# Layer 3 cross attention: TensorE's step loop written out, key parts held twice, weighted sums in one piece

## The reference

```python
q = (q_input @ W_Q + b_Q).reshape(B, LQ, 16, 8).transpose(0, 2, 1, 3)
k = (kv_input @ W_K + b_K).reshape(B, LK, 16, 8).transpose(0, 2, 1, 3)
v = (kv_input @ W_V + b_V).reshape(B, LK, 16, 8).transpose(0, 2, 1, 3)
sim = einsum('bhqd,bhkd->bhqk', q, k) / sqrt(8)
sim = where(key_padding_mask, neg_inf, sim)
out = einsum('bhqk,bhkd->bhqd', softmax(sim, axis=-1), v)
return out.reshape(B, LQ, 128) @ W_O + b_O
```

## Time and profile before

| what | us |
|---|---|
| median of 3 runs | 1829.14 |
| lowest and highest run | 1823.56, 1829.15 |
| the profiled execution, its own time | 1828.54 |
| its span in the trace | 1826.8 |
| busy in it: TensorE matmul | 1546.7 (85%) |
| busy: VectorE, ScalarE, GpSimd | 1257.7 (69%), 834.4 (46%), 321.7 (18%) |
| layer 3's steps, first row product to last weighted sum | from 1200.7 to 1673 |

### The profile page before, as it was taken

How to read it: one execution, slowest core, us unless ns; L and a number is a source line. 1 busy time by engine, 2 the same in 40 slices (tenths; PEclk the granted TensorE clock), 3 DMA queues, 4 the chain that set the end, 5 groups by cost and what they waited for, 6 DMA issues and landing times. The chain is left out here.

```text
span 1826.8 us, 40229 instructions
## 1 busy us (share of the span) xinstructions
PE 1546.7 (85%) x15246; PEld 1295.7 (71%) x15246; DVE 1257.7 (69%) x2561; ACT 834.4 (46%) x1241; POOL 321.7 (18%) x437
## 2 busy tenths in 40 slices
PE   3897397456899999999999995679898889897895
PEld 2896276336799999999999982346676667675795
DVE  4313653685788888888888873367676768785698
ACT  1332132133566666666666640335454445453332
POOL 0110000001323343323343300030000000000230
PEclk8898698667999999999999998789999999999898
DMA  2112598000211111111111000153544354450210
GB/s 40 40 35 72 125 228 195 25 9 1 68 35 35 35 36 58 40 34 34 34 36 59 6 0 6 29 139 88 121 97 111 91 118 110 99 116 8 70 36 22
DMA packets 93087, 116.02 MB, mean 64 GB/s; under 512 B 12337, under 2 KB 78306, under 8 KB 92962
## 3 DMA queue, kind: packets, MB, share of 16 engines
q1 hardware_dynamic: 92962, 114.19, 24.8%
HBM read 76.35 MB, written 0.46 MB: 42 GB/s over the span
## 5 line engine op out<-in xcount | busy, mean ns | idle before, releaser
L2306 DVE TENSOR_REDUCE l3att_parts<-PS 112x1 f32<-112x500 f32 x384 | 244.3, 671 | 104.3 <-PE PS L2049 103.3
L1728 ACT CAST l2att_PT<-PS 125x512 fp32r<-125x512 f32 x336 | 175.2, 594 | 221.1 <-PE PS L1667 221.1
L1768 DVE TENSOR_REDUCE l2att_neg<-PS 128x1 f32<-128x1500 f32 x112 | 192.7, 1721 | 77.6 <-PE PS L1660 77.6
L1774 DVE TENSOR_TENSOR l2att_PT<-PS,l2att_PT 125x512 fp32r<-125x512 f32 x336 | 210.2, 681 | 1.5 <-ACT l2att_PT L1728 1.5
L2049 PE MATMUL PS<-l3att_KS,l3att_QB 97*112 97x500 f32 x384 | 169.0, 492 | 47.0 <-issue 24.2
L2180 ACT ACTIVATE l3att_P<-PS 125x1344 f32<-125x1344 f32 x128 | 165.3, 1291 | 77.4 <-PE PS L2068 77.4
L1667 PEld LDWEIGHTS PS<-all_ident,l_P 128*125 128x125 f32 x1344 | 163.5, 187 | 14.6 <-DVE l_P L1782 6.0
L1737 ACT ACTIVATE l_P<-PS,l2att_neg 128x1500 f32<-128x1500 f32 x112 | 171.2, 1529 | 5.0 <-DVE l2att_neg L1768 5.0
L1699 PE MATMUL PS<-l2att_PT,l_cc 125*128 125x256 f32 x576 | 170.5, 296 | 0.0
L1667 PE MATMUL PS<-all_ident,l_P 128*125 128x128 f32 x1344 | 165.4, 273 | 4.3 <-DVE l_P L1782 4.3
L1701 PE MATMUL PS<-l2att_PT,l_cc 125*128 125x256 f32 x576 | 162.5, 282 | 0.0
(11 more groups left out here) (518 smaller groups left out, 2960.1 us busy)
## 6 DMA issues: line engine op xcount, KB each, us to landing
l3att_KS<-l3att_kh SPq DMA_DIRECT2D x128, 187.5 KB, 4.3
l_QP<-in_ctxT SPq DMA_DIRECT2D x8, 1500.0 KB, 11.5
l_cT<-in_ctxT SPq DMA_DIRECT2D x16, 750.0 KB
l_c<-in_ctx SPq DMA_DIRECT2D x16, 750.0 KB
l3att_cT<-in_ctxT SPq DMA_DIRECT2D x16, 750.0 KB, 4.5
l3att_KS<-l3att_kl SPq DMA_DIRECT2D x64, 187.5 KB, 4.4
l_QP<-in_ctx SPq DMA_DIRECT2D x8, 1344.0 KB
l0f_w<-in_L_ffn_W SPq DMA_DIRECT2D x16, 256.0 KB, 3.1
```

The source lines that it names most:

```text
L1728: act.copy(PT[:, 4 * g:4 * g + 4, PLACE[u1], 0, :], PS[0:CHUNK, 3 * s1 + g, :].rearrange("k (c r) -> k c r", r=128)).then_inc(hi_in, 1)
L1768: v.tensor_reduce(neg[:, s:s + 1], E, XY_AXES, ALU.max, negate=True).then_inc(top_in, 1)
L1774: v.tensor_tensor(PT[:, 4 * g:4 * g + 4, at, 1, :], PS[0:CHUNK, 3 * s1 + g, :].rearrange("k (c r) -> k c r", r=128), PT[:, 4 * g:4 * g + 4 ...
L2306: v.tensor_reduce(parts[:, u % 2, half, i:i + 1], PS[0:HROWS, PLACES[p], 0:BANK_KEYS], X_AXIS, ALU.max, negate=True).then_inc(top_in, 1)
```

## The change

1. TensorE's `one` is called in a plain Python loop over all 69 steps: its instructions are written out, with no hardware loop and no registers for waits. The other engines keep their loops.
2. `kh` and `kl` are there twice and are taken in turn by batch. ScalarE's wait at g = 0 for the transfers is gone.
3. `values` is in one piece of 48 products, between rows (4, 5) and `turned(1)`. It waits for both exponentials of its group at once.
4. Row 2 moves from ahead of `project_values` to behind it, beside row 3.

```diff
-            kh, kl = (self.sb(ctx, n, [128, KEYS], F32R) for n in ("kh", "kl"))
+            kh, kl = ([self.sb(ctx, f"{n}{s}", [128, KEYS], F32R) for s in range(2)] for n in ("kh", "kl"))
...
-                    def values(chunks):
+                    def values():
                         s, a = (u - 2) % UNROLL // SETS, (u - 2) % SETS
...
+                        pe.wait_ge(m_in, n - 1)
+                        if known is None or known >= 4:
+                            pe.wait_ge(o_in, n - 3)
+                        pe.wait_ge(vh_in, (n - 2) // SETS * BANKS + BANKS)
+                        pe.wait_ge(p_in, 2 * n - 2)
...
                     if now:
                         rows((0, 1))
-                    if before:
-                        values((0, 1, 2, 3))
                     if then:
                         maxima()
...
-                    if now:
-                        rows((2,))
                     if late or g >= 2 and more:
...
                     if now:
-                        rows((3,))
+                        rows((2, 3))
                     if then:
                         turned(0)
                     if now:
                         rows((4, 5))
                     if before:
-                        values((4, 5, 6, 7, 8, 9, 10, 11))
+                        values()
                     if then:
                         turned(1)
-                run_steps(pe, GROUPS, LAG, UNROLL, one, peeled=1)
+                for n in range(GROUPS + LAG):
+                    one(n, n % UNROLL, n)
...
                     if g < BANKS and more:
-                        if g == 0:
-                            for x in range(SETS):
-                                act.wait_ge(ks_in[u // SETS][x], n // UNROLL * 48 + 48)
-                        high_keys(act, b + 1, g, SIDE)
+                        high_keys(act, b + 1, 1 - u // SETS, g, SIDE)
```

More of the change, by code:

```diff
@@ L1964, in remap @@
                     for g in range(SETS):
-                        for r, src, done in ((0, kh, kh_in), (1, kh, kh_in), (2, kl, kl_in)):
+                        for r, src, done in ((0, kh[s], kh_in), (1, kh[s], kh_in), (2, kl[s], kl_in)):
                             sp.wait_ge(done, BANKS * b + BANKS)
@@ L2080, in maxima @@
                         mm.then_inc(t_ps, 1)
-                    def values(chunks):
+                    def values():
                         s, a = (u - 2) % UNROLL // SETS, (u - 2) % SETS
[L2084 to L2093, removed]
+                        pe.wait_ge(m_in, n - 1)
[3 more added lines that the diff above has]
+                        pe.wait_ge(p_in, 2 * n - 2)
+                        if known == 2:
+                            pe.wait_ge(blank, 1)
+                        for k in range(CHUNKS):
                             for h in range(SETS):
@@ L2097, in values @@
                                                start=k == 0, stop=k == CHUNKS - 1)
[L2098 to L2099 removed]
+                        mm.then_inc(o_ps, 1)
                     now, then, before = live(known, 0, GROUPS), live(known, 1, GROUPS), live(known, 2, GROUPS)
@@ L2158, in _ @@
                 for i in range(BANKS):
-                    high_keys(act, 0, i, i)
+                    high_keys(act, 0, 0, i, i)
                 act.wait_ge(cleared, 1)
@@ L2260, in _, with low_keys @@
                 chain = Chain(v, step)
-                def low_keys(b, i, bank):
+                def low_keys(b, s, i, bank):
                     at = slice(BANK_KEYS * i, BANK_KEYS * i + BANK_KEYS)
                     v.wait_ge(kh_in, b * BANKS + i + 1)
-                    v.scalar_tensor_tensor(out=kl[:, at], in0=PS[:, bank, 0:BANK_KEYS], scalar=bk[:, 0:1],
-                                           in1=kh[:, at], op0=ALU.add, op1=ALU.subtract).then_inc(kl_in, 1)
+                    v.scalar_tensor_tensor(out=kl[s][:, at], in0=PS[:, bank, 0:BANK_KEYS], scalar=bk[:, 0:1],
+                                           in1=kh[s][:, at], op0=ALU.add, op1=ALU.subtract).then_inc(kl_in, 1)
                 layer_norm(v, chain, XN, X, ln, 1e-5, xn_ready)
@@ L2275, in _ @@
                 for i in range(BANKS):
-                    low_keys(0, i, i)
+                    low_keys(0, 0, i, i)
                 v.wait_ge(f_ps, 1)
@@ L2318, in one @@
                     if g < BANKS and (known is None or known < GROUPS - SETS):
-                        low_keys(b + 1, g, SIDE)
+                        low_keys(b + 1, 1 - u // SETS, g, SIDE)
                     weighs = g == SETS - 1 and live(known, 2 * SETS - 1, GROUPS)
```

4 lines of the change are left out of this document (2 added, 2 removed).

## The result

| | us |
|---|---|
| kernel before, median of 4 runs beside it | 1826.35 (1817.76 to 1829.15) |
| kernel after, median of 4 runs | 1806.05 (1799.37 to 1814.89) |
| ratio after to before, 95% interval | 0.9893 [0.9865, 0.9922] |
| the profiled execution of after, its own time and its span | 1814.89, 1813.0 |

1.1% faster. The kernel after was run in two later comparisons as well: 0.986 [0.984, 0.988] and 0.9887 [0.9861, 0.9912]. Over its 15 executions the median is 1801.4. Against the kernel before beside them the three gains are 20, 26 and 22 us. The three profiled ones are 1814.89, 1812.46 and 1810.52; of the twelve others one is above 1805 (1811.21).

A forecast was written before the change was run, and what follows sets the result against it. TensorE's stalls at 5 loop turns, ScalarE's waits for `kh` transfers, and engines passing work to and fro bound the kernel. 1828.54 - 35.9 (turns, slow batches) + 5.6 (new order) + 2 (outside) = 1800.2 us; range 1782 to 1820.

The forecast's parts named there:

- The turns, -35.9: TensorE's 5 hardware-loop turns in layer 3's attention: straight code removes them and slow or long batches, 35.9 us.
- price of a turn (5.8): A batch with a turn of TensorE's loop takes 32.69 us against 26.87, so 5.8 us each.
- The order, a batch of 27.3: Four steps in the new order take 5.97, twice 6.79, and 7.75: 27.3 us against 26.87; 5.6 us over 13 batches.
- row 2's place: Row 2 behind the value projections delays VectorE's third maximum; at g = 3 it costs 0.9 us.
- the one piece: Merged weighted sums: no saving counted; 16 products behind row 5 cost 0.4 us at g = 3.
- The second buffer, -1.1 a batch: With kh and kl twice, ScalarE's wait for transfers goes and the step at g = 0 takes 1.1 us less.
- Outside the batches, +2: Steps 0 to 4 and 57 to 68, outside the 13 batches, together take about 2 us more.
- The clock falls behind the new wait: Rival: TensorE's clock falls after the 1.1 us reciprocal wait at g = 3; 1810 to 1829, chance 0.13.
- Another engine's turn: Rival: loop turns of VectorE, ScalarE and GpSimd now show; 25 us come back, 1825, chance 0.05.
- No step above 9 us: Sign in the profile after: GpSimd's starts show no step above 9 us.
- Code issued too slowly: Rival: 48-product block drains TensorE's queue, delaying `turned(1)` 0.5 us a step; 1832, chance 0.06 including a low clock.
- The order costs less, 1780: Rival: serial costs at g = 3 and other steps are hidden, batch 25.8 us, 1780; 1775 to 1790 has chance 0.17.

The follow-up runs named there:

- the run with row 2 early: Full change with row 2 back ahead of the value projections, weighted sums still in one piece; 1777.86 us, ratio 0.9726.
- two key buffers alone: Kernel before with two buffers of kh and kl and ScalarE's wait gone, loop and old order kept; 1811.01 us, ratio 0.9922.
- one key buffer: Full change with one buffer of kh and kl and ScalarE's wait at g = 0 back; 1804.46 us, ratio 0.9877.
- the two other kernels with the loop: Full change with TensorE's loop kept, 1832.21 us; kernel before with kh and kl twice and ScalarE's wait gone, 1811.01 us.
- the two straight ones with one key buffer: Kernel before with only TensorE's loop written out, 1803.82 us; full change with one buffer of kh and kl, 1804.46 us.
- the fastest order: Full change with row 2 early and sums in two pieces at g = 3 only, 1771.46 us; other engines' steps written out too, 1766.53 us.

## Why the prediction was right, and where it wasn't

The 1800 stood against 1806.05 in the first comparison, 1801.4 over all executions. The gain of 28 us was forecast and 20, 26 and 22 were measured; part of the hit is that before's median was 1824 to 1827 in these comparisons and not the 1828.5 that the sum starts from. By its own steps:

- **The turns, -35.9.** Right in size. With the second buffer the 13 batches go from 370.2 to 335.8 in the old order by straight code alone, -34.4. With one buffer they give 30.8. In the new order, the change's own, they go from 390.0 to 364.7, or to 356.3 without the 8.4 of the disturbed batch: -33.7. The prediction's price of a turn (5.8) was too low. It left out the key wait hidden in the turn, and the batch that it took (32.69) is the shortest of five; the others took up to 34.71, and the five together cost 32.3 more than 26.87 each. It took the whole 35.9 as gone for another reason (slow clocks), and that covers it.
- **The order, a batch of 27.3.** Measured 27.4, with steps of 6.04, 6.85, 6.85 and 7.67 from row 0 to row 0 against 5.97, 6.79, 6.79 and 7.75. 13 batches cost 7 us more than at 26.87, where 5.6 was forecast. The waits were where the text had them: 1.1 us for the reciprocal, 0.83 before the third maximum. Laying out the four steps from rows 6 to 8 gave each step to 0.1 us.
- **Who is to blame for it.** Here the prediction mis-sized its terms. It gave row 2's place 0.9 us at g = 3 and 0.1 at g = 1 and 2; it is 0.8 and 0.5 (the run with row 2 early). It said that the one piece saves nothing and costs 0.4 at g = 3; with row 2 early it saves 0.3 at g = 1 and 2 and does cost 0.4 at g = 3. That these errors cancel in the sum is luck. The one piece with row 2 late, against two pieces with row 2 late, wasn't run.
- **The second buffer, -1.1 a batch.** Right in the old order (25.8 against 26.87, two key buffers alone). In the full change it is nothing (one key buffer): the prediction took the wait as it was before, and didn't ask whether it would still stand in the order that it had just worked out, in which the transfers end 1.3 to 1.5 us before ScalarE wants the buffer. The step at g = 0 comes out right either way.
- **Outside the batches, +2.** The first batch gave -4.4, with steps of 6.17 and 6.04 where the kernel before had 9.20 and 7.48, and the end +7.6: +3.2 in sum. That this is near +2 is luck. Most of the -4.4 is not the change's: the two other kernels with the loop take 24.9 and 24.4 there, the two straight ones with one key buffer 25.8 and 25.6, and the profiled execution before had a granted clock of 0.52 and 0.62 from 1207 to 1223. The end took 58.9 and 60.1 in the other two profiled executions of the full change, +4.3 and +5.5 against before's 54.6. Part of the 62.2 here is the clock. At the last g = 3 the wait for the reciprocal was followed by slow work, 2.24 us for the 96 matmuls of the sums against the usual 1.37, and the granted clock from 1640 to 1663 was 0.81:

```profile
1646.90 0.45 PE L2049 MATMUL PS<-l3att_KS,l3att_QB 97*112 97x500 f32 x1 [1.08 <-DVE l3att_inv L2316]
1647.28 2.24 PE L2093 MATMUL PS<-l3att_P,l3att_VS 125*9 125x56 f32 x96
```

- **The clock falls behind the new wait.** It didn't in the twelve batches before the disturbed one. From 1225 to 1575 it is 1.00 (third number from the end), with TensorE at work in 321.54 of 350 us, and the same 1.07 to 1.1 us waits inside:

```profile
1225.00:1575.00 350.00, 321.54 (x6327) 241.19 (x6327) 272.19 (x575) 190.62 (x231) 28.43 (x51) 1.00 0.48 116
```

- **Another engine's turn.** Ruled out for the batches (the fastest order with and without the other engines' loops). The four waits in steps 53 to 55 were in no case of the prediction. "No step above 9 us" was wrong for this: one step took 10.59.
- **Code issued too slowly.** Ruled out in its form: 12.5 ns a weight load in the block of 96. The 12.7 ns that the prediction lays beside a floor for matmuls are those of weight loads; the matmuls of these blocks come every 15 ns (64 in 0.97 us) and every 14 ns (96 in 1.37 us).
- **The order costs less, 1780.** Wrong for the change as it is. But 1776 and below is what the loop and the buffers give when row 2 stays where it was.

The Trainium skill ("Runtime: NRT & Kernel Launch", Instruction fetch mechanics) has fetching of the next page in straight code run beside the work, hidden by the pace of the sequencer. Twelve batches in 13 agree. In the other the block that is due comes 4.2 to 4.8 us late in all three executions, and the fetching is not hidden; why it is late the runs don't show.

## What to carry to other kernels

Where engines pass work to and fro, write one step down as a schedule from the trace before you move an instruction: what keeps another engine fed (row 2, ahead of products that must wait for a bank anyway) goes first, and what nobody waits for (the sums) fills the waits. Price each edit in the presence of the others: a second buffer was worth 27 us in one order and nothing in another, because there the transfers had landed in time without it. And when straight code replaces a loop, look for single waits with no releaser in it, and lay them beside the starts of the code blocks, both counted from the same moment.

## What the runs showed of the hardware

- A turn of TensorE's loop of 8 steps costs 4.4 to 5.2 us of stall (15 turns in three kernels) and 6.5 to 7.6 in all where no other wait hides in it, as the clock is at its lower level behind it: the pair of rows takes 1.17 instead of 0.62. At each of the 15 turns two blocks of code start within 1.2 us of each other, and TensorE goes on 1.9 to 3.3 us behind the arrival of the second. The loops of ScalarE, VectorE and GpSimd turn at the same places and cost TensorE nearly nothing.
- Straight code brought fewer blocks of code, not more: 87 packets of the code queue in all eleven profiled executions without TensorE's loop against 98 in the three with it, since each turn fetches again. The loops of the other engines change nothing in this queue.
- In straight code TensorE waited 0.4 to 1.0 us for nothing that the profile shows, at one and the same instruction in several kernels. In the three profiled executions of one kernel it did so four times in a row, 5.9 us in sum, which made the batch 7.0 to 8.4 us longer. In every case a block of code had started late, and TensorE went on 1.3 to 1.7 us behind its arrival. What made the block late is open.
